# One-hots of the edge targets compared from int32 instead of from bf16 pairs, in a two-layer graph network kernel

## The chip, the cores and the metric

The kernel runs on one core of a Trainium2 chip. The metric is the device time of one execution in microseconds. Three runs of the kernel before gave 11010.66, 11014.35 and 11020.74 us; the median is 11014.35 us. The engines are named as in the profile: PE multiplies matrices, DVE, ACT and POOL work on vectors, SP issues DMAs. POOL also issues the indirect gathers.

## The reference

There are 12,500 nodes with 16 features and 412,500 edges, sorted by target. Two layers follow each other, each closed by a residual sum and a layer norm.

```python
# layer 0: 90 relation types, matrices W_rel from 30 bases
h_src = h[src]
e = concat([h_src @ Ws.T, he @ Ws.T, h[dst] @ Ws.T]) @ Wa.T      # one score for each edge
msg = einsum('ei,eio->eo', h_src, W_rel[rel_type]) * e
x = layernorm(x + segment_sum(msg, dst))
# layer 1: 8 edge types, message by a matrix for each type, then a GRU cell
m = segment_sum(einsum('emh,eh->em', A[edge_type], x[src]), dst)
x = layernorm(x + gru(m, x))
```

## The kernel before

Each of the 128 partitions owns a run of consecutive edges. The edges are worked off in 52 chunks of 62 edges for each partition (CHUNK = 62), two chunks to a pair, with two buffers of everything. First a table is built in HBM that holds, for every node and relation type, the transformed row (`relation_table`). Of the 62 edges of a chunk in layer 0, 44 get their row out of that table: POOL issues one indirect DMA for each of these 44 columns (`gather`, L480), which takes one row for each partition by the int32 offsets in `idx`. The other 18 edges (`Layer.share`) are computed: PE multiplies one-hots with the node features and the relation matrices, ACT makes these one-hots, and DVE picks and sums the products (`make_rows`, L1118 to L1132). They come in a first group of two and four groups of four, the five "quads" of a chunk, counted here 0 to 4.

DVE weighs the rows of a chunk with the edge scores and sums over runs of equal targets with scans (`scan`, L1082). In DVE's program the work of chunk n is woven between the quads of chunk n+1 (`with_quad`). At quad 0 stand `target_parts` and `edge_scores`, at quad 1 `weigh_messages`, whose first instruction (the index for chunk n+2, L1015) stands behind the wait for the landed gathers of chunk n. Scans are spread over quads 1 to 4.

The change touches a side computation: a histogram of the targets, which later gives the last row of each node. `target_parts` takes the low 7 bits of the 62 targets (`dst_lo_i`) and the rest (`dst_hi_i`) as int32, and casts both to bf16 (`dst_lo`, `dst_hi`). `target_hots` then compares them with 0, 1, 2, ... (`iota_bf`), for 16 edges at a time (14 in the last), one instruction for the low part, 128 wide, and one for the high part, 98 wide. I call these two instructions a pair of compares. There are four in a chunk, one at each of the quads 1 to 4 (HOT_WITH), and each stands behind that quad's scans. PE multiplies the two one-hots into `ps_hist` (L610). All operands are stored as pairs: the innermost dimension of `hot_lo`, `hot_hi` and `iota_bf` is 2 and runs over two neighbouring edges, so that every operand has two bf16 values side by side.

POOL runs ahead. While DVE works on chunk n, POOL issues the gathers of chunk n+1, and it goes on to chunk n+2 when the offsets of that chunk are set and the buffer is free. Nothing in POOL's program waits for the compares. In the last chunk the four pairs of compares stand one behind the other, before its wait for the gathers.

The order of each engine's instructions is written out by hand; semaphores connect the engines.

Of the kernel before, what the change touches and what calls it, by code (L numbers as in the profile page):

```python
# [41 lines left out]
def build(nc, x, src, dst, edge_attr, type_8, type_90, Ws, Wa, weight, w_comp,  # L42
# [44 lines left out]
    with ctx:  # L87
        def sb(name, shape, dt=F32):
            return ctx.enter_context(nc.sbuf_tensor(name, shape, dt))
# [36 lines left out]
        run_start = sb("run_start", [P, 1], I32)  # L126
        iota_bf = sb("iota_bf", [P, P, 2], BF16)
        zeros_bf = sb("zeros_bf", [P, P], BF16)
# [50 lines left out]
        dst_hi_i = sb("dst_hi_i", [P, CHUNK], I32)  # L179
        dst_lo = sb("dst_lo", [P, CHUNK], BF16)  # L180
        dst_hi = sb("dst_hi", [P, CHUNK], BF16)
        hot_lo = sb("hot_lo", [P, 2, HOT // 2, P, 2], BF16)
        hot_hi = sb("hot_hi", [P, 2, HOT // 2, TILES, 2], BF16)
        ordered = sb("ordered", [P, 4])
# [371 lines left out]
        def _(pe):  # L556
# [49 lines left out]
            def count_edges(i, q):  # L606

                pe.wait_ge(hot_set[q % 2], i * HOTS + q // 2 + 1)
                for k in range(min(HOT, CHUNK - q % HOTS * HOT)):
                    last = pe.matmul(ps_hist[0:TILES, 0:P], hot_hi[:, q % 2, k // 2, :, k % 2],  # L610
                                     hot_lo[:, q % 2, k // 2, :, k % 2],
                                     start=False, stop=False)
                last.then_inc(hot_used[q % 2], 1)
# [318 lines left out]
        def _(dve):  # L932
# [48 lines left out]
            dve.wait_ge(consts_set, 2)  # L981
            dve.tensor_copy(iota_bf[:, :, :], iota_i[:, :].unsqueeze(2).to_broadcast([P, P, 2]))
            dve.tensor_copy(ident_bf[:, :], ident[:, :])
# [177 lines left out]

            STEPS = 5

# [3 lines left out]
            def target_parts(i, h):  # L1167
# [5 lines left out]
                chunk_done(i, h, 1)  # L1173
                dve.tensor_copy(dst_lo[:, :], dst_lo_i[:, :])
                dve.tensor_copy(dst_hi[:, :], dst_hi_i[:, :]).then_inc(chunk_step, 1)
                chunk_done(i, h, 2)

            def target_hots(i, h, q):

                b = (h * HOTS + q) % 2  # L1180
                wait_past(dve, hot_used[b], i * HOTS + (h * HOTS + q) // 2)
                edges = slice(q * HOT, min((q + 1) * HOT, CHUNK))
                twos = (edges.stop - edges.start) // 2
                for hot, part, width in ((hot_lo, dst_lo, P), (hot_hi, dst_hi, TILES)):
                    all_of = [P, twos, width, 2]
                    last = dve.tensor_tensor(hot[:, b, 0:twos, :, :],  # L1186
                                             part[:, edges].rearrange("p (c e) -> p c e", e=2).unsqueeze(2).to_broadcast(all_of),
                                             iota_bf[:, 0:width, :].unsqueeze(1).to_broadcast(all_of), ALU.is_equal)
                last.then_inc(hot_set[b], 1)

            def edge_scores(i, h):
# [3 lines left out]
                                  he_w[:, :].unsqueeze(1).to_broadcast([P, CHUNK, D]), ALU.mult).then_inc(chunk_step, 1)  # L1195
                chunk_done(i, h, 3)
                dve.tensor_reduce(score[:, :], he_dot[:, :, :], AX, ALU.add).then_inc(he_used[h], 1)

            def weigh_messages(i, h):
# [5 lines left out]
                dve.tensor_tensor(score[:, :], score[:, :], rows0[:, h, :, D], ALU.add).then_inc(chunk_step, 1)  # L1205
                chunk_done(i, h, 4)
                dve.tensor_tensor(weighted[:, :, :], rows0[:, h, :, 0:D],
                                  score[:, :].unsqueeze(2).to_broadcast([P, CHUNK, D]), ALU.mult
                                  ).then_inc(chunk_step, 1)
                wait_past(dve, scan0_out[h], i * 16)  # L1210
                chunk_done(i, h, 5)

# [304 lines left out]
```

## Time and profile before

| | |
|---|---|
| median of three runs | 11014.35 us (11010.66 to 11020.74) |
| span of the profiled execution, first to last instruction | 6658.0 us |
| outside the span (median less span) | 4356.35 us |
| PE, PEld busy | 5232.2, 4919.8 us |
| DVE busy | 4394.2 us (66%) |
| ACT busy | 4410.5 us (66%) |
| POOL busy | 5012.1 us (75%) |
| layer 0, the chunks | about 250 to 3590 us of the span |
| layer 1, the chunks | about 3730 to 6500 us |

The profiled execution has no other time of its own than its span; what lies outside (launch and the like) the trace does not show. Busy shares are averages over stages with different limits, so they are to be read by stage. An indirect gather of POOL is one row in the trace; its duration is the time until POOL is through with it, not until the data have landed.

### The profile page before, as it was taken

How to read it: one execution, taken by the hardware profiler on the slowest of the kernel's cores; microseconds unless marked ns; L12 is line 12 of the kernel's file. 1: busy time of each engine (PE TensorE's matmuls, PEld its weight loads, DVE VectorE, ACT ScalarE, POOL GpSimd, SP SyncE). 2: the span in 40 equal slices, each digit the busy share in tenths (PEclk: the TensorE clock that was granted, in tenths of full speed). 3: DMA queues.
4: the chain of work that ended last, by engine and by line, in shares of the span. 5: the costliest groups of instructions: out<-in, count | busy, mean ns of one | idle time of the engine just before them, and what ended most of it. 6: DMA issues, size and time to landing. Idle time of an engine off the chain costs nothing.

```text
span 6658.0 us, 145553 instructions
## 1 busy us (share of the span) xinstructions
PE 5232.2 (79%) x56854; PEld 4919.8 (74%) x56854; DVE 4394.2 (66%) x9230; ACT 4410.5 (66%) x5373; POOL 5012.1 (75%) x4786
## 2 busy tenths in 40 slices
PE   5687786777777778777784889898888988898884
PEld 1476676776777667677673789888888988888883
DVE  2477676676766767667674566676666666666663
ACT  5775665665666566566562678777777877777763
POOL 5477777777777777777776677777777777777776
PEclk7798898888889888888886799999999999999995
DMA  9511111111111111111112121212122122222221
GB/s 309 209 35 26 35 33 27 35 25 35 32 29 35 26 35 32 28 35 25 35 32 44 36 18 17 17 17 18 17 19 19 17 17 17 17 17 18 20 17 13
DMA packets 647456, 248.56 MB, mean 37 GB/s; under 512 B 531458, under 2 KB 620379, under 8 KB 646360
## 3 DMA queue, kind: packets, MB, share of 16 engines
q0 software_dynamic: 152992, 41.40, 7.9%
q10 hardware_dynamic: 421728, 84.39, 7.3%
q1 hardware_dynamic: 72152, 113.41, 5.1%
q8 instruction: 559, 9.16, 0.6%
q14 instruction: 25, 0.20, 0.0%
HBM read 75.13 MB, written 163.34 MB: 36 GB/s over the span
## 4 chain that ended last, share of the span: by engine, by line
POOL 72%; issue 22%; DMA 3%; ACT 1%; DVE 1%; ACTq 0%; POOLq 0%; PE 0%; SPq 0%; DVEq 0%
POOL rows L480 70%; DMA relation_table<-scanned 2%; POOL sums L480 2%; DMA sums<-scanned,group_row 0%; ACT scanned L817 0%; ACTq L806 0%; DMA relation_table<-t_buf 0%; DMA scanned<-scanned 0%; DVE scanned L1082 0%; DMA scanned<-carry,fix_row 0%; DMA x_sb<-in_x 0%; POOLq L478 0%; ACT t_buf L817 0%; DVE whole L966 0%; PE ps_table L752 0%
## 5 line engine op out<-in xcount | busy, mean ns | idle before, releaser
L647 PE MATMUL ps_table<-node_parts,hot_key 128*128 128x192 bf16 (+1 forms) x44928 | 4173.0, 256 | 756.2 <-DVE by_in L1127 750.9
L647 PEld LDWEIGHTS ps_table<-node_parts,hot_key 128*128 128x128 bf16 x44928 | 3970.7, 101 | 843.2 <-DVE by_in L1127 751.8
L845 ACT ACTIVATE hot_key<-ps_misc,less_key 128x512 bf16<-128x512 f16 x3744 | 2214.0, 702 | 1906.3 <-PE ps_misc L623 1901.7
L480 POOL DMA_INDIRECT rows<-relation_table,idx x2288 | 2626.5, 1148 | 773.4 <-issue 697.0
L480 POOL DMA_INDIRECT rows<-type_table,idx x2184 | 2097.1, 960 | 681.7 <-issue 665.2
L850 ACT ACTIVATE hot_key<-hot_key,ones 128x3072 bf16<-128x3072 bf16 (+1 forms) x468 | 1513.9, 3235 | 15.2
L1123 DVE TENSOR_REDUCE source<-picked 128x32 f32<-128x416 f32 x936 | 805.1, 860 | 32.2
L1132 DVE TENSOR_REDUCE rows<-by_in 128x32 f32<-128x512 f32 (+1 forms) x988 | 694.1, 703 | 33.8
L1118 DVE TENSOR_TENSOR picked<-ps_table,hot_tile 128x416 f32<-128x416 f32 x936 | 543.8, 581 | 250.6 <-PE ps_table L657 250.0
L1127 DVE TENSOR_TENSOR by_in<-ps_table,source 128x512 f32<-128x512 f32 (+1 forms) x936 | 660.9, 706 | 32.3
L1140 DVE TENSOR_SCALAR hot_key<-hot_key 128x1024 bf16<-128x1024 bf16 x260 | 117.5, 452 | 680.3 <-ACT hot_type L846 680.3
L1015 DVE SCALAR_TENSOR_TENSOR idx<-src_sb,t_sb 128x44 int32 (+3 forms) x108 | 21.9, 205 | 787.6 <-DMA rows<-relation_table,idx 598.5
L623 PE MATMUL ps_misc<-ident_f,match_cols 128*128 128x128 f16 x3848 | 325.3, 228 | 201.5 <-issue 150.3
L623 PEld LDWEIGHTS ps_misc<-ident_f,match_cols 128*128 128x128 f16 x3848 | 265.4, 102 | 240.0 <-issue 168.6
L1082 DVE TENSOR_TENSOR_SCAN scanned<-cont,scanned,rows 128x62 f32<-128x62 f32 x1664 | 423.9, 327 | 2.0
L657 PE MATMUL ps_table<-rel_mats,hot_type 90*128 90x272 bf16 x2496 | 358.0, 279 | 0.0
L846 ACT ACTIVATE hot_type<-ps_misc,less_type 96x512 bf16<-96x512 f16 (+1 forms) x468 | 330.7, 707 | 0.0
L610 PE MATMUL ps_hist<-hot_lo,hot_hi 128*98 128x128 bf16 x3224 | 223.9, 221 | 66.2 <-DVE hot_hi L1186 66.1
L610 PEld LDWEIGHTS ps_hist<-hot_lo,hot_hi 128*98 128x98 bf16 x3224 | 209.9, 124 | 77.4 <-DVE hot_hi L1186 74.6
L657 PEld LDWEIGHTS ps_table<-rel_mats,hot_type 90*128 90x128 bf16 x2496 | 236.0, 97 | 32.4
L1186 DVE TENSOR_TENSOR hot_lo<-dst_lo,iota_bf 128x2048 bf16<-128x2048 bf16 x208 | 242.5, 1166 | 0.0
L480 POOL DMA_INDIRECT sums<-scanned,group_row x196 | 185.4, 946 | 68.3 <-issue 58.8
(197 smaller groups left out, 2527.5 us busy)
## 6 DMA issues: line engine op xcount, KB each, us to landing
scanned<-scanned ACTq DMA_DIRECT2D x52, 992.0 KB, 3.9
relation_table<-scanned SPq DMA_DIRECT2D x50, 765.0 KB, 6.4
relation_table<-t_buf SPq DMA_DIRECT2D x48, 765.0 KB, 6.5
rows<-relation_table,idx POOLq DMA_INDIRECT x2288
rows<-type_table,idx POOLq DMA_INDIRECT x2184
scanned<-scanned ACTq DMA_DIRECT2D x52, 496.0 KB, 8.3
he<-in_edge_attr SPq DMA_DIRECT2D x52, 434.0 KB
type_table<-t_buf SPq DMA_DIRECT2D x14, 448.0 KB, 3.0
```

The costliest lines, as they stand in the source:

```text
L480: pool.indirect_dma_start(out=rows[:, k, :], out_offset=None, in_=table, in_offset=bass.IndirectOffsetOnAxis(ap=index[:, k:k + 1], axis=0) ...
L610: last = pe.matmul(ps_hist[0:TILES, 0:P], hot_hi[:, q % 2, k // 2, :, k % 2], hot_lo[:, q % 2, k // 2, :, k % 2], start=False, stop=False)
L623: last = pe.transpose(match_bank[:, k, c * P:(c + 1) * P], match_cols[:, parity, k, at:at + 1].to_broadcast([P, P]), ident_f16[:, :])
L647: pe.matmul(ps_table[duo][:, 0, t * BLOCK_W:t * BLOCK_W + width], hot_key[:, b, g, edges], node_parts[:, part, g:TILES:BLOCKS, :], start=( ...
L657: last = pe.matmul(ps_table[duo][:, 1 + t, 0:lay.outs * D], hot[:, edges], mats_part, start=(k == 0), stop=(k == len(lay.mats) - 1))
L845: act.activation(hot_key[:, b, g, :], match_bank[:, 0, :], ACT.Abs, bias=less_key[:, g:g + 1])
L850: last = act.activation(hot_key[:, b, 0:last_block, :], hot_key[:, b, 0:last_block, :], ACT.Relu, bias=ones[:, 0:1], scale=-1.0)
L1082: return dve.tensor_tensor_scan(scanned[:, h, :, at + f], cont[:, :], messages[:, :, f], scanned[:, 1 - h, CHUNK - 1, at + f:at + f + 1], ...
L1118: dve.tensor_tensor(picked[:, :, :, :], ps_table[duo][:, 0, 0:DUO * BLOCK_W].rearrange("p (t j f) -> p t j f", t=DUO, f=D), hot_tile[:, ha ...
L1123: dve.tensor_reduce(source[:, :, :], picked[:, :, :, :].rearrange("p t j f -> p t f j"), AX, ALU.add).then_inc(match_step[lay.n], 1)
L1127: dve.tensor_tensor(by_in[:, :, 0:lay.outs, :], ps_table[duo][:, 1:1 + DUO, 0:lay.outs * D].rearrange("p t (o i) -> p t o i", i=D), source ...
L1132: dve.tensor_reduce(lay.rows[:, half, lay.own + own:lay.own + own + DUO, 0:lay.outs], by_in[:, :, 0:lay.outs, :], AX, ALU.add).then_inc(ro ...
```

## The change

The casts to bf16 and the bf16 iota go. The compares read the int32 parts and the int32 iota that the kernel has anyway, and their outputs are stored edge by edge, still in bf16. The number of compares, their elements and their places stay. PE reads the one-hots with unit stride. The step count of a chunk falls from 5 to 4.

```diff
@@ -177,10 +176,8 @@
         dst_lo_i = sb("dst_lo_i", [P, CHUNK], I32)
         dst_hi_i = sb("dst_hi_i", [P, CHUNK], I32)
-        dst_lo = sb("dst_lo", [P, CHUNK], BF16)
-        dst_hi = sb("dst_hi", [P, CHUNK], BF16)
-        hot_lo = sb("hot_lo", [P, 2, HOT // 2, P, 2], BF16)
-        hot_hi = sb("hot_hi", [P, 2, HOT // 2, TILES, 2], BF16)
+        hot_lo = sb("hot_lo", [P, 2, HOT, P], BF16)
+        hot_hi = sb("hot_hi", [P, 2, HOT, TILES], BF16)
...
                 for k in range(min(HOT, CHUNK - q % HOTS * HOT)):
-                    last = pe.matmul(ps_hist[0:TILES, 0:P], hot_hi[:, q % 2, k // 2, :, k % 2],
-                                     hot_lo[:, q % 2, k // 2, :, k % 2],
+                    last = pe.matmul(ps_hist[0:TILES, 0:P], hot_hi[:, q % 2, k, :], hot_lo[:, q % 2, k, :],
                                      start=False, stop=False)
...
             dve.wait_ge(consts_set, 2)
-            dve.tensor_copy(iota_bf[:, :, :], iota_i[:, :].unsqueeze(2).to_broadcast([P, P, 2]))
...
                 chunk_done(i, h, 1)
-                dve.tensor_copy(dst_lo[:, :], dst_lo_i[:, :])
-                dve.tensor_copy(dst_hi[:, :], dst_hi_i[:, :]).then_inc(chunk_step, 1)
-                chunk_done(i, h, 2)
...
                 edges = slice(q * HOT, min((q + 1) * HOT, CHUNK))
-                twos = (edges.stop - edges.start) // 2
-                for hot, part, width in ((hot_lo, dst_lo, P), (hot_hi, dst_hi, TILES)):
-                    all_of = [P, twos, width, 2]
-                    last = dve.tensor_tensor(hot[:, b, 0:twos, :, :],
-                                             part[:, edges].rearrange("p (c e) -> p c e", e=2).unsqueeze(2).to_broadcast(all_of),
-                                             iota_bf[:, 0:width, :].unsqueeze(1).to_broadcast(all_of), ALU.is_equal)
+                count = edges.stop - edges.start
+                for hot, part, width in ((hot_lo, dst_lo_i, P), (hot_hi, dst_hi_i, TILES)):
+                    all_of = [P, count, width]
+                    last = dve.tensor_tensor(hot[:, b, 0:count, :], part[:, edges].unsqueeze(2).to_broadcast(all_of),
+                                             iota_i[:, 0:width].unsqueeze(1).to_broadcast(all_of), ALU.is_equal)
```

On DVE, the start of a chunk's side work before the change (quad 0 of the first pair; `dst_lo_i` and `dst_hi_i` are the int32 parts of the targets):

```order
L1170 TENSOR_SCALAR dst_lo_i<-dst_sb 128x62
L1171 TENSOR_SCALAR dst_hi_i<-dst_sb 128x62
L1174 CAST dst_lo<-dst_lo_i 128x62
L1175 CAST dst_hi<-dst_hi_i 128x62
L1076 SCALAR_TENSOR_TENSOR cont<-dst_sb,ordered 128x62
L1194 TENSOR_TENSOR he_dot<-he,he_w 128x992
L1197 TENSOR_REDUCE score<-he_dot 128x62
```

The same place on DVE after the change:

```order
L1165 TENSOR_SCALAR dst_lo_i<-dst_sb 128x62
L1166 TENSOR_SCALAR dst_hi_i<-dst_sb 128x62
L1071 SCALAR_TENSOR_TENSOR cont<-dst_sb,ordered 128x62
L1185 TENSOR_TENSOR he_dot<-he,he_w 128x992
L1188 TENSOR_REDUCE score<-he_dot 128x62
```

Two instructions a chunk are gone, and the lines behind have moved up by five and more. The second place is quad 1 on DVE, with the first pair of compares (`hot_lo`, `hot_hi`) between the scans and the next picked rows, before:

```order
L1207 TENSOR_TENSOR he_dot<-rows,score 128x992
L1082 SCALAR_TENSOR_TENSOR scanned<-cont,scanned,rows 128x62 x4
L1186 TENSOR_TENSOR hot_lo<-dst_lo,iota_bf 128x2048
L1186 TENSOR_TENSOR hot_hi<-dst_hi,iota_bf 128x1568
L1118 TENSOR_TENSOR picked<-ps_table,hot_tile 128x416
L1123 TENSOR_REDUCE source<-picked 128x32
```

The same place on DVE after the change:

```order
L1198 TENSOR_TENSOR he_dot<-rows,score 128x992
L1077 SCALAR_TENSOR_TENSOR scanned<-cont,scanned,rows 128x62 x4
L1178 TENSOR_TENSOR hot_lo<-dst_lo_i,iota_i 128x2048
L1178 TENSOR_TENSOR hot_hi<-dst_hi_i,iota_i 128x1568
L1113 TENSOR_TENSOR picked<-ps_table,hot_tile 128x416
L1118 TENSOR_REDUCE source<-picked 128x32
```

The compares keep their places and sizes and read the int32 tiles; POOL's, ACT's, SP's and PE's instructions stand in the same order as before.

## Rows read from the trace of the kernel before

**Rows 1.** The page: span, and the chain that ended last, by line.
```profile
span 6658.0 us, 145553 instructions
...
POOL rows L480 70%; DMA relation_table<-scanned 2%; POOL sums L480 2%; DMA sums<-scanned,group_row 0%; ACT scanned L817 0%; ACTq L806 0%; DMA relation_table<-t_buf 0%; DMA scanned<-scanned 0%; DVE scanned L1082 0%; DMA scanned<-carry,fix_row 0%; DMA x_sb<-in_x 0%; POOLq L478 0%; ACT t_buf L817 0%; DVE whole L966 0%; PE ps_table L752 0%
```

**Rows 2.** Groups by shape, POOL's gathers: count | busy us, mean ns | idle before
```profile
L480 POOL DMA_INDIRECT rows<-relation_table,idx x2288 | 2626.5, 1148 | 773.4 <-issue 697.0 <-DMA relation_table<-scanned 76.4
L480 POOL DMA_INDIRECT rows<-type_table,idx x2184 | 2097.1, 960 | 681.7 <-issue 665.2 <-DMA type_table<-t_buf 16.4
```

**Rows 3.** Timeline, DVE, first instruction behind the gathers' landing, in consecutive chunks
```profile
2039.69 0.20 DVE L1015 SCALAR_TENSOR_TENSOR idx<-src_sb,t_sb 128x44 int32 x1 [14.68 <-DMA rows<-relation_table,idx]
...
2103.97 0.20 DVE L1015 SCALAR_TENSOR_TENSOR idx<-src_sb,t_sb 128x44 int32 x1 [7.92 <-DMA rows<-relation_table,idx]
```

**Rows 4.** Waits over the span: engine, line <- releaser: us, times, longest
```profile
PE ps_table L647 <- DVE by_in L1127: 750.9, 78, 16.7
...
DVE idx L1015 <- DMA rows<-relation_table,idx: 598.5, 50, 16.0
...
DVE picked L1118 <- PE ps_table L657: 250.0, 164, 13.9
```

**Rows 5.** Groups by shape, DVE's compares of the targets and one cast
```profile
L1186 DVE TENSOR_TENSOR hot_lo<-dst_lo,iota_bf 128x2048 bf16<-128x2048 bf16 x156 | 187.1, 1200 | 0.0
...
L1186 DVE TENSOR_TENSOR hot_hi<-dst_hi,iota_bf 128x1568 bf16<-128x1568 bf16 x156 | 150.9, 967 | 0.0
...
L1186 DVE TENSOR_TENSOR hot_lo<-dst_lo,iota_bf 128x1792 bf16<-128x1792 bf16 x52 | 55.3, 1064 | 0.0
...
L1186 DVE TENSOR_TENSOR hot_hi<-dst_hi,iota_bf 128x1372 bf16<-128x1372 bf16 x52 | 44.9, 864 | 0.0
...
L1174 DVE CAST dst_lo<-dst_lo_i 128x62 bf16<-128x62 int32 x52 | 13.6, 261 | 1.8
```

**Rows 6.** Groups by shape, DVE's other two-tensor instructions, 32-bit operands
```profile
L1194 DVE TENSOR_TENSOR he_dot<-he,he_w 128x992 f32<-128x992 f32 x52 | 61.6, 1184 | 0.0
...
L1098 DVE TENSOR_TENSOR hot_tile<-match_i,iota_i 128x234 f32<-128x234 int32 x52 | 20.6, 396 | 0.0
```

**Rows 7.** Timeline (start, duration), a gather beside one f32 product of DVE
```profile
2019.70 1.18 DVE L1194 TENSOR_TENSOR he_dot<-he,he_w 128x992 f32<-128x992 f32 x1
...
2020.26 1.44 POOL L480 DMA_INDIRECT rows<-relation_table,idx  x1 [0.30 <-issue]
```

**Rows 8.** Timeline, a free gather, then gathers beside the chunk's four compare pairs
```profile
2010.87 0.94 POOL L480 DMA_INDIRECT rows<-relation_table,idx  x1 [0.30 <-issue]
2012.12 2.86 POOL L480 DMA_INDIRECT rows<-relation_table,idx  x1 [0.30 <-issue]
...
2042.31 1.20 DVE L1186 TENSOR_TENSOR hot_lo<-dst_lo,iota_bf 128x2048 bf16<-128x2048 bf16 x1
2042.42 2.80 POOL L480 DMA_INDIRECT rows<-relation_table,idx  x1 [0.30 <-issue]
2043.43 0.97 DVE L1186 TENSOR_TENSOR hot_hi<-dst_hi,iota_bf 128x1568 bf16<-128x1568 bf16 x1
...
2053.15 2.67 POOL L480 DMA_INDIRECT rows<-relation_table,idx  x1 [0.30 <-issue]
...
2060.51 0.59 DVE L1118 TENSOR_TENSOR picked<-ps_table,hot_tile 128x416 f32<-128x416 f32 x1 [2.60 <-PE ps_table L657]
...
2064.88 4.33 POOL L480 DMA_INDIRECT rows<-relation_table,idx  x1 [0.30 <-issue]
```

**Rows 9.** Timeline, a compare of f32 output from int32, and the gather beside it
```profile
2112.06 0.40 DVE L1098 TENSOR_TENSOR hot_tile<-match_i,iota_i 128x234 f32<-128x234 int32 x1
2112.30 0.97 POOL L480 DMA_INDIRECT rows<-relation_table,idx  x1 [0.30 <-issue]
```

**Rows 10.** Timeline of the last chunk: the last of four compare pairs in a row
```profile
3561.82 1.08 DVE L1186 TENSOR_TENSOR hot_lo<-dst_lo,iota_bf 128x1792 bf16<-128x1792 bf16 x1
...
3562.14 1.58 POOL L480 DMA_INDIRECT rows<-relation_table,idx  x1 [0.30 <-issue]
```

More of the change, by code:

```diff
@@ L126, in build @@
         run_start = sb("run_start", [P, 1], I32)
-        iota_bf = sb("iota_bf", [P, P, 2], BF16)
         zeros_bf = sb("zeros_bf", [P, P], BF16)
@@ L1158, in chunk_rows @@
                         between(q)
-            STEPS = 5
+            STEPS = 4
             def chunk_done(i, h, k):
@@ L1195, in edge_scores @@
                                   he_w[:, :].unsqueeze(1).to_broadcast([P, CHUNK, D]), ALU.mult).then_inc(chunk_step, 1)
-                chunk_done(i, h, 3)
+                chunk_done(i, h, 2)
                 dve.tensor_reduce(score[:, :], he_dot[:, :, :], AX, ALU.add).then_inc(he_used[h], 1)
@@ L1205, in weigh_messages @@
                 dve.tensor_tensor(score[:, :], score[:, :], rows0[:, h, :, D], ALU.add).then_inc(chunk_step, 1)
-                chunk_done(i, h, 4)
+                chunk_done(i, h, 3)
                 dve.tensor_tensor(weighted[:, :, :], rows0[:, h, :, 0:D],
@@ L1210, in weigh_messages @@
                 wait_past(dve, scan0_out[h], i * 16)
-                chunk_done(i, h, 5)
+                chunk_done(i, h, 4)
             def scan_some(h, some):
```

## The prediction

> **What bounds the kernel now.** I read the chain that ended last first. POOL's gathers at L480 are 70% of it; the reader is to see that no other line has more than 2% [rows 1]. So layers 0 and 1 go at the pace at which POOL gets through its indirect gathers. Then the groups by shape: a gather of layer 0 takes 1148 ns in the mean and one of layer 1 takes 960, and POOL is idle in front of them for 697.0 us over 2288 gathers, 0.305 us each, which nothing but the issue itself explains [rows 2]. So POOL never waits for DVE once it has begun; a chunk of layer 0 should take 44 times (0.94 + 0.305), about 55 us. The timeline says 64.3 us from one landing to the next (2039.69 to 2103.97) [rows 3]. Where do the missing 9 us go?
>
> The timeline beside single gathers answers that. A free one takes 0.94 us. Those that run into a pair of compares take 2.86, 2.80, 2.67 and 4.33 [rows 8]. Take the second: the gather starts at 42.42 (of 2042.42), `hot_hi` ends at 43.43 + 0.97 = 44.40, and the gather ends at 45.22, 0.82 later. The same arithmetic holds for a plain f32 product: it ends at 2019.70 + 1.18 = 2020.88 and the gather at 2021.70, again 0.82 later [rows 7]. I read this so: about 0.12 us after its start a gather needs something that DVE holds during an instruction with two inputs in SBUF; it gets it when DVE's instruction ends, and then needs its last 0.82 us. Of the four pairs, a pair delays one gather by 1.92, 1.86, 1.73 and 3.39 us in the rows shown, 8.9 us a chunk. From the groups: 2288 x (1148 - 944) ns is 467 us, 9.0 us a chunk, and the f32 product adds 0.5 of it in the chunk of rows 7. So the compares cost POOL, and thereby the kernel, some 8 us a chunk, 415 us in all, though DVE itself has time to spare.
>
> DVE waits 598.5 us for gathers, 11.5 us a chunk, and 250.0 us for PE; PE waits 750.9 us for DVE [rows 4]. Those engines are not the bound: their chain takes 64 - 11.5 = 52.5 us of a chunk's 64.
>
> **The change part by part.** *The compares' own time.* In bf16 pairs, 2048 elements take 1200 ns and 1792 take 1064, so 0.53 ns an element; 1568 and 1372 take 967 and 864 [rows 5]. No row shows these shapes from int32 with a bf16 output. The nearest is `hot_tile`, also an is_equal of an int32 part against the int32 iota with the same kind of broadcast, f32 out: 234 elements in 396 ns; the f32 product takes 1184 ns for 992 [rows 6]. Between the two the slope is 788/758 = 1.04 ns an element with 153 ns fixed. I take this line: 2048 elements 2.28 us, 1568 1.78, 1792 2.02, 1372 1.58. A full pair grows by 1.08 + 0.82 = 1.90 us, the short one by 0.95 + 0.72 = 1.67, a chunk by 3 x 1.90 + 1.67 = 7.37 us. Lower bound: the old time (growth 0, if the 16-bit output let it run at 0.53). [...] All 32-bit rows lie on the line, so I take it.
>
> [...]
>
> *What lies beside other work.* On DVE itself the 7.37 us fall into its wait of 11.5 us for the gathers. Two casts of 0.26 us or less go, about 0.5 us a chunk, into the same wait [rows 5]. DVE and PE would need 52.5 + 7.4 - 0.5 = 59.4 us a chunk, under the present 64. If POOL's cover were gone this would be the period. PE counts the edges behind the fourth pair, so it may wait up to 1.7 us more there once a chunk; it idles for 750.9 us anyway.
>
> *What lies on the path.* A pair outlasts the period of a gather, 1.25 us, both before (2.08 us with the overlap of its two) and after (3.98 us), so one gather is always caught, and is let go at the pair's end. Every us that the pair gets longer is a us that this gather gets longer, and all later ones start later. So POOL's chunk grows by the full 7.37 us, to 71.4, above the 59.4 of DVE and PE. In 51 chunks this is 376 us. In the last chunk the four pairs stand in a row and gathers slip through between them (below): I take 3 us for it. Bounds for this holding: none (0) and whole (379 us).
>
> *Phase.* How long a gather is caught depends also on where it stands when the scans and the pair begin. The third pair holds one for 3.39 us, since it is caught in the scans ahead of it. In front of that pair DVE waits 2.60 us for PE [rows 8]; with two longer pairs, less PE's own delay by the first, some 1.9 us of this wait go, so the meeting point moves. If the third pair then held only as the others do (1.84 before the growth), that is 1.55 x 52 = 81 us less; if the fourth were caught early as well, 1.47 x 52 = 76 us more. Nothing tells which; the third is now near the worst case, so I take a quarter of the loss, -20 us.
>
> *Startup.* The iota cast goes: under 1 us, taken as nothing. PE's reads of the one-hots are now of unit stride, off the path either way. Layer 1 has no compare and stays.
>
> Sum: 376 + 3 - 20 = 359 us. The span goes from 6658 to 7017 us. Laid onto the median, with the 4356 us outside the span unchanged: 11014 + 359 = 11373 us.
>
> [...]
>
> **The rivals.** *A, gathers slip through between `hot_lo` and `hot_hi`.* In the last chunk a gather started at 3562.14 and took 1.58 us, so it was let go at 3562.90, the end of `hot_lo` (61.82 + 1.08), not of `hot_hi` [rows 10]. If the longer compares left that gap each time, the next gather would start inside the pair and only the rest of `hot_hi` would hold it: one period of 1.25 us is saved in each of the 204 other pairs, 255 us, and 359 - 255 = 104 us remain: 11118 us. Against: in all four pairs of rows 8 the gather was held to the end of the second compare.
>
> *B, the time hides.* The compares' growth falls into DVE's 11.5 us and POOL is held no longer than now. For: the chain charges DVE with almost nothing, and the stall does not appear as a wait anywhere. It needs holds of a fixed length; the f32 product's hold followed its own end. 11014 us.
>
> [...]
>
> [...]
>
> **How the numbers follow.** Forecast 77%, A 10%, B 5%, C 5%, D 3%. The forecast's own range is 359 with the phase from -81 to +76 (less the -20 taken): 298 to 455, so 11310 to 11470, and somewhat lower for a mixture with A. With A's 11118 and a margin for its phase the range reaches from 11100 to 11460. B, C and D are left out. A difference within 0.2% (22 us) can't be told from none. Slower: the forecast, A and D, 90%. Same: B, 5%. Faster: C, 5%.
>
> **What would show it.** After the change: (1) `hot_lo` of 2048 in 2.28 us and `hot_hi` of 1568 in 1.78; (2) the mean gather of layer 0 at 1148 + 7.37/44 us = 1.31 us, that of layer 1 at 0.96; (3) 71 us between landings; (4) DVE's wait for gathers still about 11 us a chunk; (5) caught gathers of 4 to 5 us, which end 0.82 us behind a pair. I am wrong if caught gathers end behind `hot_lo` (A), keep their length (B), or are 0.94 beside the compares with POOL waiting for offsets or buffers (C).

## The result and the profile after

Before: 11015.53 us (4 runs, 11010.66 to 11020.74). After: **11211.7 us** (4 runs, 11197.34 to 11216.88). The ratio is 1.018, interval 1.0165 to 1.0194: slower by 196 us, clear of the noise, where 359 us had been forecast.

The first thing to read is the span of the page after, and its chain by engine:

```profile
span 11215.1 us, 145400 instructions
...
PE 26%; another core or an unknown queue 26%; issue 24%; DVE 21%; ACT 2%; DMA 1%; DVEq 0%; ACTq 0%; POOL 0%; SPq 0%; POOLq 0%
```

The span is 11215.1 us, and the timed run it belongs to took 11216.88 us: 1.8 us lie outside the span, not 4356. And POOL, 70% of the chain of before [rows 1], has 0% here. So the trace of before had caught an execution of another kind: 6658 us, where the timed runs took 11014. The unchanged kernel, run again with a profile (the first experiment below), shows the same two things:

```profile
span 11020.7 us, 145553 instructions
...
PE 50%; issue 41%; ACT 4%; another core or an unknown queue 3%; DMA 1%; DVE 1%; SPq 0%; POOL 0%; ACTq 0%; DVEq 0%; POOLq 0%
```

So both kernels have **two levels**. Before took 11026 and 11223 us on two chips and 6657 and 6650 us on two others; on each of them all its executions lie within 0.2% of their median. Each chip was used in one session only, so the record can't tell a property of the chip from one of the session; nor does it name the chip of the trace of [rows 1] or of the first timed runs. Ratios and differences below are between kernels on one chip. Only after's trace of the upper level stands beside traces from a chip that may be another, on which before takes nearly the same (11026 us for 11016).

*What the upper level is.* Both kinds have the same instructions, but in the upper one PE slows down once in nearly every one of the 104 chunks. Timeline of after, PE inside such a stretch (start and duration in us; in brackets the idle time before, which nothing but PE's own issue explains):

```profile
2557.62 0.28 PE L653 MATMUL ps_table<-rel_mats,hot_type 90*128 90x272 bf16 x1 [0.44 <-issue]
2558.34 0.28 PE L653 MATMUL ps_table<-rel_mats,hot_type 90*128 90x272 bf16 x1 [0.44 <-issue]
2559.04 0.28 PE L653 MATMUL ps_table<-rel_mats,hot_type 90*128 90x272 bf16 x1 [0.43 <-issue]
```

Here one matmul starts every 0.70 us. Each lasts 0.28 us, no longer than its kind does in the trace of before (0.28 us in the mean), and PE idles 0.44 us in front of it: the matmuls themselves are not slower, they come later. Further into the stretch the steps are of 0.70 or of 1.4 us. Cut a chunk of layer 0 into three: PE at full pace beside the first gathers, the slow stretch, and the rest. Of after:

```profile
core 0: us, PE busy (x) PEld busy (x) DVE busy (x) ACT busy (x) POOL busy (x), PEclk, DMA share, GB/s
2531.00:2556.00 25.00, 20.53 (x229) 19.17 (x227) 23.80 (x40) 14.75 (x20) 20.51 (x13) 0.93 0.15 46
2556.00:2601.00 45.00, 9.50 (x32) 3.17 (x32) 0.00 (x0) 4.46 (x3) 29.71 (x32) 0.54 0.11 18
2601.00:2631.00 30.00, 26.54 (x276) 25.07 (x276) 29.07 (x53) 19.61 (x24) 0.22 (x1) 0.89 0.01 2
```

Of before at the same level (first experiment), the same three:

```profile
1787.00:1815.00 28.00, 22.36 (x217) 20.28 (x215) 19.92 (x38) 13.68 (x20) 22.51 (x19) 0.82 0.22 60
1815.00:1852.00 37.00, 6.54 (x20) 1.97 (x19) 0.00 (x0) 6.40 (x6) 24.09 (x26) 0.54 0.10 8
1852.00:1880.00 28.00, 27.00 (x301) 25.95 (x301) 25.48 (x53) 19.20 (x23) 0.20 (x1) 0.93 0.00 1
```

In the middle part of after PE has 32 matmuls and 32 weight loads in 45 us, one instruction per 0.70 us in the mean, where it does 229 and 227 in the 25 us ahead. DVE has none. POOL alone goes on, a gather each 1.25 us. In the last third POOL is idle and PE, DVE and ACT catch up. The gathers of the next chunk wait for that, so POOL now has a wait that [rows 2] did not have:

```profile
L477 POOL DMA_INDIRECT rows<-relation_table,idx x2288 | 2598.0, 1135 | 2684.5 <-DVE scanned L1077 1821.1 <-issue 682.0 <-DMA relation_table<-scanned 181.3
```

The granted clock is 0.54 in the middle part and 0.93 and 0.89 beside it; over the span it is 0.720 in after and 0.715 in before at this level, against 0.874 in the execution of [rows 1]. The stretches with gathers are not all of the difference: before's first gather of layer 0 starts at 355.9 us here for 252.8 in [rows 1]'s trace, and between the gathers of the two layers lie 272.4 us for 164.0.

*What of the prediction shows directly.* The compares by shape, answering to [rows 5]:

```profile
L1178 DVE TENSOR_TENSOR hot_lo<-dst_lo_i,iota_i 128x2048 bf16<-128x2048 int32 x156 | 353.6, 2266 | 0.0
L1178 DVE TENSOR_TENSOR hot_hi<-dst_hi_i,iota_i 128x1568 bf16<-128x1568 int32 x156 | 278.3, 1784 | 0.0
L1178 DVE TENSOR_TENSOR hot_lo<-dst_lo_i,iota_i 128x1792 bf16<-128x1792 int32 x52 | 103.9, 1999 | 0.0
L1178 DVE TENSOR_TENSOR hot_hi<-dst_hi_i,iota_i 128x1372 bf16<-128x1372 int32 x52 | 82.1, 1579 | 0.0
```

And the gathers that they catch, answering to [rows 8], in the chunk of the windows above (timeline: start, duration):

```profile
2531.83 5.82 POOL L477 DMA_INDIRECT rows<-relation_table,idx  x1 [35.47 <-DVE scanned L1077]
2532.86 2.27 DVE L1178 TENSOR_TENSOR hot_lo<-dst_lo_i,iota_i 128x2048 bf16<-128x2048 int32 x1
2535.04 1.79 DVE L1178 TENSOR_TENSOR hot_hi<-dst_hi_i,iota_i 128x1568 bf16<-128x1568 int32 x1
...
2544.25 4.55 POOL L477 DMA_INDIRECT rows<-relation_table,idx  x1 [0.30 <-issue]
...
2594.22 0.95 POOL L477 DMA_INDIRECT rows<-relation_table,idx  x1 [0.31 <-issue]
...
2630.78 5.82 POOL L477 DMA_INDIRECT rows<-relation_table,idx  x1 [35.62 <-DVE scanned L1077]
```

The first gather starts while the scans ahead of the pair still run (until 2532.95), and is held through them and through the pair: it ends at 2537.65, 0.82 us behind the end of `hot_hi` at 2536.83. Only two of a chunk's four pairs meet gathers here; the other two start at 2606.73 and 2619.23, while POOL stands idle. Over the whole trace 100 of the 208 pairs meet gathers, and each of these has a gather that ends 0.81 to 0.83 us behind it.

### The profile page after: what moved, and what is told of

It is laid out like the page before. It is cut to its first block, busy times and chain, and to the rows that moved or that the text cites. A ratio compares the mean times of both kernels' runs of the same rounds, so it can differ in the third digit from the quotient of the medians.

```text
span 11215.1 us, 145400 instructions
## 1 busy us (share of the span) xinstructions
PE 6092.2 (54%) x56854; PEld 5053.0 (45%) x56854; DVE 4745.5 (42%) x9125; ACT 4412.5 (39%) x5373; POOL 4952.6 (44%) x4786
## 4 chain that ended last, share of the span: by engine, by line
PE 26%; another core or an unknown queue 26%; issue 24%; DVE 21%; ACT 2%; DMA 1%; DVEq 0%; ACTq 0%; POOL 0%; SPq 0%; POOLq 0%
PE ps_table L643 22%; DVE scanned L1077 3%; DVE hot_lo L1178 3%; DVE hot_hi L1178 3%; DVE source L1118 3%; DVE by_in L1122 3%; DVE picked L1113 2%; PE ps_table L653 2%; PE ps_misc L619 1%; DVE rows L1127 1%; ACT hot_key L841 1%; DMA relation_table<-scanned 1%; DVE he_dot L1198 1%; DVE he_dot L1185 1%
## 5 line engine op out<-in xcount | busy, mean ns | idle before, releaser
L643 PE MATMUL ps_table<-node_parts,hot_key 128*128 128x192 bf16 (+1 forms) x44928 | 4838.0, 262 | 3832.5 <-issue 3660.9
L643 PEld LDWEIGHTS ps_table<-node_parts,hot_key 128*128 128x128 bf16 x44928 | 4048.0, 102 | 4550.6 <-issue 4286.1
L477 POOL DMA_INDIRECT rows<-relation_table,idx x2288 | 2598.0, 1135 | 2684.5 <-DVE scanned L1077 1821.1
L477 POOL DMA_INDIRECT rows<-type_table,idx x2184 | 2065.4, 946 | 3194.5 <-DVE scanned L1077 2513.2
L619 PE MATMUL ps_misc<-ident_f,match_cols 128*128 128x128 f16 x3848 | 367.6, 235 | 343.0 <-issue 292.2
L653 PE MATMUL ps_table<-rel_mats,hot_type 90*128 90x272 bf16 x2496 | 425.4, 296 | 224.2 <-issue 222.9
L1178 DVE TENSOR_TENSOR hot_lo<-dst_lo_i,iota_i 128x2048 bf16<-128x2048 int32 x208 | 457.5, 2200 | 0.0
L1178 DVE TENSOR_TENSOR hot_hi<-dst_hi_i,iota_i 128x1568 bf16<-128x1568 int32 x208 | 360.4, 1733 | 0.0
L607 PE MATMUL ps_hist<-hot_lo,hot_hi 128*98 128x128 bf16 x3224 | 257.8, 232 | 158.0 <-DVE hot_hi L1178 108.6
```

Source lines behind the costliest of these rows:

```text
L477: pool.indirect_dma_start(out=rows[:, k, :], out_offset=None, in_=table, in_offset=bass.IndirectOffsetOnAxis(ap=index[:, k:k + 1], axis=0) ...
L619: last = pe.transpose(match_bank[:, k, c * P:(c + 1) * P], match_cols[:, parity, k, at:at + 1].to_broadcast([P, P]), ident_f16[:, :])
L643: pe.matmul(ps_table[duo][:, 0, t * BLOCK_W:t * BLOCK_W + width], hot_key[:, b, g, edges], node_parts[:, part, g:TILES:BLOCKS, :], start=( ...
L653: last = pe.matmul(ps_table[duo][:, 1 + t, 0:lay.outs * D], hot[:, edges], mats_part, start=(k == 0), stop=(k == len(lay.mats) - 1))
L1178: last = dve.tensor_tensor(hot[:, b, 0:count, :], part[:, edges].unsqueeze(2).to_broadcast(all_of), iota_i[:, 0:width].unsqueeze(1).to_bro ...
```

## The experiments

Times of kernels are medians. "A chunk" is a chunk of layer 0. Its parts are medians over the chunks of one trace unless called means: the gathers' time from the first to the last; in it the *hold*, the sum of what gathers take over 0.945 us; then the time until PE is back at full pace; and the *rest* from there to the next gathers. The recorded expectations speak of the runs by their labels: e1 to e6 are the experiments 1 to 6, e8, e9, e10 and e11 the experiments 7 to 10, e13 and e14 the experiments 11 and 12. "Kernel 9" is the kernel of experiment 9.

**1. Before, unchanged.**

> The kernel before, unchanged. The trace of after has a span of 11215 us and in each of the 104 chunks one stretch of 43 to 53 us in which PE issues one instruction every 0.70 us; the trace of before that I predicted from has a span of 6658 us and no such stretch. Theory S (the stretches belong to every timed execution of both kernels, and the trace of before was of an execution without them): the span is about 11013 us, with some 103 stretches, POOL idles 30 us or more a chunk in front of its gathers for DVE's scans, and a chunk of layer 0 takes about 95 us (98.9 less 196/52 = 3.8). Rival O (the 4356 us lie outside the span, and the change brought the stretches): the span is 6658 us again, without stretches.

11027.49 us against 11026.26, ratio 1.0001 (0.999 to 1.0011), span 11020.7. So the timed level belongs to the program, not to what lies around it, and the trace of [rows 1] shows a different level. A chunk is 94.9 us: gathers 59.2 with 4.6 of hold (both means), the stretch ending 5.9 behind the last gather, rest 29.5. In after it is 98.9: gathers 63.4 with 8.7 of hold, 5.8, rest 29.65. By the means a chunk takes 3.9 us more, which is 195 us in 50 chunks. Summed over layer 0, the gathers take 199 us more than in experiment 1's trace, and POOL's long waits in front of them (over 0.5 us) are the same, 2002.5 us for 2002.9. So the 196 us stand in the gathers, and there they are hold.

**2 and 3. Only the pairs 1 and 2 from int32; only the pairs 3 and 4.** Both are before with

```
+        INTS = (0, 1)        # the third experiment: (2, 3)
...
+                    if q in INTS:
+                        all_of = [P, count, width]
+                        last = dve.tensor_tensor(ones_of(hot, b, width)[:, 0:count, :],
+                                                 part_i[:, edges].unsqueeze(2).to_broadcast(all_of),
+                                                 iota_i[:, 0:width].unsqueeze(1).to_broadcast(all_of), ALU.is_equal)
+                        continue
```

> Only the first and second pair of compares of each chunk (at quads 1 and 2) read int32 in the layout of after; the third and fourth stay bf16 pairs; the casts stay. Theory D (DVE and PE take turns, and only pairs between which PE has nothing left to do are on the path): after is 196 us or 3.8 us a chunk slower, two pairs' growth of 1.9; the first pair stands behind the slow stretch where PE waits 2.6 us for it, so this gets one full growth and perhaps half of the second: +100 to +150 us. Theory P (my prediction: every pair holds a gather and POOL is the bound): half of 196, +98 us, each pair the same.

> The mirror: only the third and fourth pair read int32. Theory D: the rest of the 196 us, +50 to +100 us, with PE's waits for the fourth pair 1.7 us longer. Theory P: +95 us (3.57 of 7.37 parts of 196).

Both expectations missed: they had +98 to +150 us for pairs 1 and 2, and +50 to +100 for pairs 3 and 4. Pairs 1 and 2: 11041.84 us, ratio 1.0013 (1.0004 to 1.0023), +16. Pairs 3 and 4: 10994.51, ratio 0.9967 (0.9955 to 0.998), so 32 us *faster*. Pairs 3 and 4 do what they should to the gathers (63.9 us a chunk, hold 9.25), but the rest falls from 29.5 to 25.6 us and takes the loss back. Together the two parts make -16 us, the whole change +196: at this level costs do not add.

**4. All four pairs from int32, the pair layout and the casts kept.**

```
-                for hot, part, width in ((hot_lo, dst_lo, P), (hot_hi, dst_hi, TILES)):
+                for hot, part, width in ((hot_lo, dst_lo_i, P), (hot_hi, dst_hi_i, TILES)):
...
-                                             iota_bf[:, 0:width, :].unsqueeze(1).to_broadcast(all_of), ALU.is_equal)
+                                             iota_i[:, 0:width].unsqueeze(2).unsqueeze(1).to_broadcast(all_of), ALU.is_equal)
```

> All compares read int32, but write the one-hots in the pair layout of before, so that PE reads them with a stride of two as before; the casts and the bf16 iota stay, unused. Theory L (the layout that PE reads costs or gives nothing): within 0.3% of after, ratio 1.018 against before. Rival (PE's unit stride gives back part of it): slower than after, 1.02 or more. Rival (the scattered 16-bit writes of DVE cost more): hot_lo over 2.3 us, 1.02 or more.

11087.27 us, ratio 1.0047 (1.0029 to 1.0065), +61: under what any of its theories said. `hot_lo` takes 2267 ns in the mean, for 2266 in after, so writing in pairs costs DVE nothing here. Gathers 63.8 us and hold 9.2 (after: 63.4 and 8.7); the rest is near 29.7 us in every second chunk and mostly about 26 in the others.

The four kernels at this level side by side, each trace against that of experiment 1, in us:

| | POOL's time in gathers, layer 0 | POOL's long waits, layer 0 | whole span |
|---|---|---|---|
| pairs 1 and 2 | +58 | -54 | +7 |
| pairs 3 and 4 | +246 | -255 | -10 |
| all, layout and casts kept | +272 | -203 | +75 |
| after | +199 | 0 | +194 |

The first column is the hold, and it is paid in all four. What differs is how much of it the waits give back.

**5. Compares of two elements.** This kernel leaves out all but two elements of each compare, and with them nearly all of the histogram. It and the next three ran on a chip at the lower level (before: 6656.96 us), so what they were expected to say of the upper level stays open.

```
+                    last = dve.tensor_tensor(hot[:, b, 0, 0, :], part[:, q * HOT:q * HOT + 2], iota_bf[:, 0, :],
+                                             ALU.is_equal)
```

> From before: each compare works on 2 elements in place of 1372 to 2048, so the histogram is wrong from here on; all waits, casts and PE's 62 products a chunk stay. It asks what the compares cost in timed executions. Model M, from the traces of the unchanged kernel run again and of after: a chunk of layer 0 = time from the first to the last gather (55.0 us + what DVE's instructions hold, 4.6 in before, 8.7 in after) + 5.8 us until PE's slow stretch ends + the rest until DVE has scanned the rows and the next gathers start (29.2 and 29.7 us). With M and a hold of some 0.8 us the gathers take 56 us; the rest is PE's left-over work of 28 us or more and shrinks little: period 90 to 92.5 us, -110 to -240 us. Rival P (my prediction, POOL always busy): the hold of 8 us a chunk goes, -415 us. Rival Z (the compares cost nothing, 11026 us, and after's 196 us come from the new layout alone).

6340.04 us, ratio 0.9526 (0.951 to 0.9542). The hold falls from 9.2 to 1.8 us a chunk and the period from 64.2 to 56.7. The chunks of layer 0 take 378 us less; the prediction had put the compares' cost before any change at 415. Between the gathers of the two layers 57 us more pass, 221 for 164, which was not looked into, and 317 us remain as the gain of the whole.

**6. The weighing, some scans and the first pair moved to quad 0.**

```
-        HOT_WITH, COUNT_WITH = ((), (0,), (1,), (2,), (3,)), ((), (), (0,), (1,), (2, 3))
+        HOT_WITH, COUNT_WITH = ((0,), (), (1,), (2,), (3,)), ((), (), (0,), (1,), (2, 3))
...
-            SCAN_WITH = (range(0), range(4), range(4, 12), range(12, 24), range(24, 2 * D))
+            SCAN_WITH = (range(4), range(4, 8), range(8, 16), range(16, 24), range(24, 2 * D))
```

> From before, bf16 pairs as they are: the weighing of the landed rows, 4 scans and the first pair of compares move from quad 1 to quad 0 in DVE's program, so in front of DVE's long wait for PE's slow stretch, and the scans of the rows end one quad earlier (at quad 2), which lets the next gathers start earlier. Theory D (DVE's chain sets the rest of the chunk behind the slow stretch): 4.9 us of DVE work hide in the 5.8 us between the gathers' end and the end of the slow stretch, -250 us or more. Rival W (PE's left-over work sets it): the next gathers start earlier but the slow stretch starts earlier too, by the same time, and within 0.5% of before.

6609.6 us, ratio 0.9932 (0.9916 to 0.9949). The hold is 8.2 us in place of 9.2. This order shifts the hold by 1 us a chunk; that the pairs are there at all makes most of it, by experiment 5.

**7. The gathers cut in two bursts,** the second from the 23rd on, behind PE's first products of quad 1.

```
+            CUTS = (((22, 1, 0),), ())
...
+                            pool.wait_ge(products_ps[lay.n],
+                                         i * (2 * lay.duos) + lay.done(h, q, duo))
```

> From before: in layer 0 POOL issues 22 of a chunk's 44 gathers and then waits until PE has finished the first products of quad 1 of that chunk, before it issues the other 22. Layer 1 is unchanged. Theory G (PE's slow stretch is tied to the gathers: it begins 6 to 20 us after they begin and ends 5.8 us behind the last): the stretch of 45 us breaks into two of some 13 us, or ends 6 us behind the 22nd gather, and a chunk gets 10 to 20 us shorter, 10000 to 10500 us in all. Rival I (the stretch belongs to a place in PE's instruction stream or in its loop and only happens to lie beside the gathers): it stays 45 us long while POOL stands still, and the chunk gets longer by the wait, slower than 11100 us.

6658.26 us, ratio 1.0004 (0.9994 to 1.0014). In the trace the 23rd gather waits 3.4 us in the first chunk, and in the other 51 no longer than without the edit, 0.3 us. It was meant to break the slow stretches; the chip had none, so it tells nothing of them. A miss.

**8. After, with the two casts put back.**

```
+                dve.tensor_copy(dst_lo[:, :], dst_lo_i[:, :])
+                dve.tensor_copy(dst_hi[:, :], dst_hi_i[:, :]).then_inc(chunk_step, 1)
```

> From after: the two casts of the target parts to bf16 and their wait stay (0.5 us a chunk), only nobody reads them. With e4 (int32 compares in the pair layout, casts kept, +61 us) this tells what the 150 us between e4 and after are: if the layout that PE reads, this is at after's time, 1.018 of before or 0.5 us a chunk more; if the missing casts, which move DVE's work against the slow stretch, it is near e4, 1.005.

7053.24 us, ratio 1.0599 (1.0581 to 1.0616), **+396 us**.

**9 and 10. After again, and after with its iota in PSUM.** A second chip at the lower level (before: 6649.77 us). The tenth kernel keeps int32 targets and unpacked outputs, but one of the two inputs, the iota, is no longer in SBUF; it lies as f32 in PSUM, the memory that PE writes to. For that the compares have moved behind DVE's wait for the products of the bank in which the iota lies, so their place in DVE's program differs too.

```
+        iota_ps = ps_table[1][:, 1, 512 - P:512]
...
                     dve.wait_ge(products_ps[lay.n], lay.done(m, q, duo))
+                    if duo == 1:
+                        owned(q)
...
-                                             iota_i[:, 0:width].unsqueeze(1).to_broadcast(all_of), ALU.is_equal)
+                                             iota_ps[:, 0:width].unsqueeze(1).to_broadcast(all_of), ALU.is_equal)
```

> The kernel after, unchanged. The kernel before has now been timed at two levels: about 11015 to 11026 us, with PE's slow stretches, and 6657 us, without them. At 11015 us the change cost 196 us. At 6657 us only the variant with the casts kept has run, +396 us. Theory P (without the slow stretches POOL is the bound and each us that a pair of compares grows holds a gather one us longer; the casts lie in DVE's wait): where before takes 6657 us, after takes 7040 to 7055 us, ratio 1.058 to 1.060. Rival (the casts matter there too): more than 10 us off e9's 7053. Where before takes 11020 us: 1.018 again.

> From after: the iota that the compares read lies in a free part of one of PE's product banks in PSUM (as f32), so each compare has only one input in SBUF; for that the pairs of compares move behind DVE's wait for the second products of their quad. Where before takes 6657 us: theory H (what holds a gather is an instruction with two inputs in SBUF, however long it takes) has the hold fall from 16.8 us a chunk to 1 to 2 us though the compares last 2.3 and 1.8 us; POOL would need 56.5 us a chunk and DVE with PE, whose wait gets longer by the pairs, 58 to 62: 6350 to 6600 us. Rival T (it is the length of DVE's instruction that counts, or its writes): the hold stays near 16 us and the time near 7050. Where before takes 11020 us: model M has the gathers' time fall from 63.4 to 57 us and the rest grow by up to 4: 10850 to 11100 us.

After: 7039.75 us, ratio 1.0587 (1.0569 to 1.0604), **+390 us**. With the iota in PSUM: 6287.42, ratio 0.9454 (0.9438 to 0.947), 362 us *under* before and 752 under after. That is faster even than the 6350 to 6600 us that theory H gave. The groups of after and then of the PSUM kernel:

```profile
L477 POOL DMA_INDIRECT rows<-relation_table,idx x2288 | 3006.8, 1314 | 773.1 <-issue 696.9 <-DMA relation_table<-scanned 76.2
```

```profile
L479 POOL DMA_INDIRECT rows<-relation_table,idx x2288 | 2254.6, 985 | 773.7 <-issue 697.0 <-DMA relation_table<-scanned 76.8
...
L1182 DVE TENSOR_TENSOR hot_lo<-dst_lo_i,ps_table 128x2048 bf16<-128x2048 int32 x156 | 353.0, 2263 | 3.2 <-PE ps_table L655 3.2
```

The compare itself is as long as with two SBUF inputs (2263 ns for 2266), only the gathers go free. One pair in the timeline of after:

```profile
2025.96 2.27 DVE L1178 TENSOR_TENSOR hot_lo<-dst_lo_i,iota_i 128x2048 bf16<-128x2048 int32 x1
2026.07 4.68 POOL L477 DMA_INDIRECT rows<-relation_table,idx  x1 [0.30 <-issue]
2028.14 1.79 DVE L1178 TENSOR_TENSOR hot_hi<-dst_hi_i,iota_i 128x1568 bf16<-128x1568 int32 x1
```

And one of the PSUM kernel:

```profile
2018.48 2.26 DVE L1182 TENSOR_TENSOR hot_lo<-dst_lo_i,ps_table 128x2048 bf16<-128x2048 int32 x1
2018.59 0.94 POOL L479 DMA_INDIRECT rows<-relation_table,idx  x1 [0.30 <-issue]
2019.84 0.94 POOL L479 DMA_INDIRECT rows<-relation_table,idx  x1 [0.30 <-issue]
2020.66 1.78 DVE L1182 TENSOR_TENSOR hot_hi<-dst_hi_i,ps_table 128x1568 bf16<-128x1568 int32 x1
2021.09 0.94 POOL L479 DMA_INDIRECT rows<-relation_table,idx  x1 [0.30 <-issue]
```

Both gathers start 0.11 us behind `hot_lo`. The first takes 4.68 us and ends at 2030.75, 0.82 behind the pair's end (2029.93); the second takes 0.94. The same holds over both traces. In kernel 9 all 208 pairs are followed by the end of a gather, 0.81 to 0.83 us behind them. In kernel 10's layer 0 a compare runs 0.11 us behind the start of 572 gathers (119 in kernel 9, half of them of 4.55 us or more), and the longest of the 572 takes 0.96 us. So the moved place of the compares does not explain it: they meet more gathers than in kernel 9 and hold none.

**11 and 12. The second and the tenth kernel on a chip at the upper level** (before: 11222.69 us).

> The kernel of e2 (from before; only the first and second pair of a chunk read int32), which cost 14 us where before takes 11026. Where before takes 6650 us: theory P has each pair's growth on POOL, 2 x 1.90 us x 51 chunks = 194 us, half of after's 390. Rival (after's cost lies in the later pairs or is not additive): under 120 or over 270 us. Where before takes 11020 us: +14 us again, and then this says only that e2 repeats.

> The kernel of e11, run again for its time on another chip if it comes to one. Where before takes 6650 us: 0.945 again. Where before takes 11020 us: model M, 0.985 to 1.007.

Pairs 1 and 2 from int32: 11161.24 us, ratio 0.9942 (0.9925 to 0.9958), so -61 us here and +16 on the first chip. The PSUM kernel: 11714.08, ratio 1.0435 (1.0418 to 1.0453), *slower* by 491 us, where model M gave 0.985 to 1.007, and with the gathers freer than anywhere:

```profile
L479 POOL DMA_INDIRECT rows<-relation_table,idx x2288 | 2220.1, 970 | 3473.7 <-DVE scanned L1079 2610.0 <-issue 681.7 <-DMA relation_table<-scanned 182.0
```

```profile
1731.00:1741.00 10.00, 8.32 (x99) 7.80 (x98) 8.35 (x13) 9.08 (x11) 7.87 (x8) 1.00 0.07 5
1741.00:1794.00 53.00, 9.12 (x34) 3.73 (x34) 4.32 (x12) 0.52 (x1) 34.59 (x37) 0.54 0.14 26
1794.00:1840.00 46.00, 37.77 (x406) 35.15 (x405) 39.24 (x65) 29.69 (x35) 0.03 (x1) 0.86 0.05 13
```

These are the three parts of one of its chunks, under the same headings as above. The same of kernel 11, on the same chip:

```profile
1723.00:1744.00 21.00, 17.58 (x211) 16.23 (x208) 19.72 (x38) 14.72 (x20) 17.34 (x13) 1.00 0.19 55
1744.00:1789.00 45.00, 10.64 (x38) 3.56 (x36) 0.00 (x0) 4.48 (x3) 29.65 (x32) 0.51 0.13 18
1789.00:1819.00 30.00, 26.59 (x296) 25.16 (x297) 29.16 (x53) 20.08 (x24) 0.29 (x1) 0.94 0.01 2
```

The slow stretch begins 10 us behind the first gather of kernel 12 and 21 behind that of kernel 11. So PE has done less by then, 99 matmuls for 211, and has 406 left for the time behind it, for 296. By the medians the gathers are 4.4 us shorter than in kernel 11 (55.8 for 60.2), the stretch ends 6.4 us behind the last gather (for 5.9), the rest is 14.2 us longer (44.0 for 29.8), and the chunk takes 106.2 us for 95.8. These two kernels differ in more than the gathers, though. In kernel 12 the compares stand behind DVE's wait for PE, and three of the four pairs fall into the rest, where kernel 11 has two; all four are int32, the outputs are unpacked and the casts gone. After did not run on this chip, so how much of the loss comes from the free gathers and how much from the place of the compares was not separated.

## Why the prediction was right and wrong

**The mechanism: right.** A compare with both inputs in SBUF holds a gather until it ends, and the gather ends 0.82 us later. The kernels 9 and 10 show it: a compare of the same length (2266 and 2263 ns), one input elsewhere, and the mean gather goes from 1314 to 985 ns. It takes both inputs in SBUF: with the iota in PSUM none of 572 gathers beside a compare took over 0.96 us. Compares of 16-bit parts at 0.53 ns an element [rows 5, rows 8] and of 32-bit parts at 1.1 ns both do it. The 0.12 us of the prediction shows at DVE's f32 products (`he_dot`) in the trace of [rows 1]. The 82 gathers that start inside a product, 0.21 us or more before its end, all end 0.81 to 0.82 us behind that end. The 5 that start 0.11 us before the end take 0.94, as free ones do, and so do 87 in which the product begins 0.18 us or more behind their start (0.96 at most). Between the two, a gather that starts 0.16 us before the end of an int32 compare takes 0.97 us and ends 0.81 behind it [rows 9]. What it is that DVE holds no trace names; that stays the prediction's reading.

**The sizes: right, at the level they were read from.** By the prediction's own points:
1. `hot_lo` 2266 ns (2.28 forecast), `hot_hi` 1784 (1.78), the short ones 1999 and 1579 (2.02 and 1.58).
2. Mean gather of layer 0 1314 ns (1.31), of layer 1 962 (0.96).
3. The two landings here are 71.85 us apart (71):

```profile
2023.35 0.20 DVE L1010 SCALAR_TENSOR_TENSOR idx<-src_sb,t_sb 128x44 int32 x1 [11.75 <-DMA rows<-relation_table,idx]
...
2095.20 0.20 DVE L1010 SCALAR_TENSOR_TENSOR idx<-src_sb,t_sb 128x44 int32 x1 [17.51 <-DMA rows<-relation_table,idx]
```

4. DVE's wait for gathers 737.7 us, 14.2 a chunk and not 11: rather than fill that wait, the change made it longer. POOL's chunk grew by 7.4 us and DVE's work by 6.9 (7.4 less the casts), and DVE waited less for PE, 149.0 us in place of 250.0 [rows 4], 1.9 a chunk; so by this sum 2.4 more were left to wait for gathers, and 2.7 were measured. An error without a price, since DVE stayed off the path.
5. Caught gathers of mostly 4.55 us and up to 5.99 (4 to 5 forecast), ending 0.82 behind a pair.

The hold grew from 9.2 to 16.6 us a chunk, 7.4 for the 7.37 of the sum, and the chunks of layer 0 take 380 us more than in the trace of [rows 1]. On the two chips of this level the change (with the casts kept on one) costs 390 and 396 us against the 359. The -20 for the phase did not come: 376 + 3 = 379 without it is within 11 us of 390.

**The step that failed** is the last sentence of the sum: "Laid onto the median, with the 4356 us outside the span unchanged". The timed executions had no such 4356 us; in every profiled run since, 1.8 us or less lie outside the span. They had a slow stretch in nearly every chunk, and POOL stands idle in front of each chunk's gathers, for 35.5 us in the rows above, so "the gathers are the path" holds for part of the chunk only. The sign of it stood beside the span: 11014 us timed, 6658 traced. The sum should have been laid onto the traced execution alone, or given with a second case for the timed one.

**That 11212 us fell into the stated range was luck.** The forecast's own range, 11310 to 11470 us, begins 98 us above it. The stated range reached down to 11100 only for rival A, and A hardly happened: of the 100 pairs that meet gathers in after's trace, 2 let one go at `hot_lo`'s end. The slow stretches, which did bring the time down, stood in no part of the sum.

**Where 163 of the 359 us went.** At the upper level two of the four pairs fall into the part of the chunk where no gather runs. There the windows show PE as busy as DVE: before 27.00 and 25.48 of 28 us, after 26.54 and 29.07 of 30. The growth of pairs 1 and 2, 3.8 us, fills DVE's slack and moves the rest by 0.2 us. Pairs 3 and 4 still meet gathers; their growth of 1.90 + 1.67 = 3.57 us is nearly all of the measured 3.9 a chunk. This says where the time stands in the trace. It is not what a pair costs alone, as experiments 2 and 3 show. With the change the chain that ended last has also moved in part to DVE: PE 50%, issue 41% and DVE 1% in before at this level, PE 26% and DVE 21% in after.

**What kept that from being a rule.** The parts do not add (experiments 2, 3, 4, 11), and 12 turns the sign. What goes with the gains and losses is how much PE gets done before the slow stretch begins and how much it has left behind it. Of some 534 matmuls a chunk, kernel 3 has 265 left and a rest of 25.6 us, before 309 and 29.5, kernel 11 305 and 29.8, kernel 12 410 and 44.0. After has 292 and 29.65, with DVE busy for nearly all of it. A reading that fits, argued from the traces and not tested: a long-held gather at the burst's start leaves PE time for more work before POOL's undisturbed gathers begin, and what PE has not done by then it does later, with POOL idle. Queue q8, which the profile calls `instruction`, may have to do with the stretch itself. Its packets and share of the 16 DMA engines, in the first 25 us of after's chunk:

```profile
q10 hardware_dynamic: 144, 1.02, 9.8%
q0 software_dynamic: 370, 0.10, 4.9%
q8 instruction: 2, 0.03, 0.5%
```

In the 45 us of the slow stretch it has no row at all:

```profile
q0 software_dynamic: 1038, 0.28, 7.3%
q1 hardware_dynamic: 160, 0.51, 3.8%
```

In the 30 us behind it there are three packets again. The same holds for after's layer 0 throughout: none of 49 stretches has such a packet. But in before at this level 17 of 49 have some, in kernel 12 23 of 49, and in layer 1 of each trace 24 of 49, and the stretch goes on all the same. So this is a correlation and no proof. At the lower level, beside the gathers of a 72 us chunk of kernel 9, q8 has 5 packets and there is no stretch; whether it has a part in the stretches of the upper level was not shown.

**The rivals.** A, slipping between the two compares: rare. In kernel 9 each of the 208 pairs holds a gather to its end; only in the last chunk (all 4) and at 8 of the 204 other pairs was one let go at `hot_lo`'s end before that. B, the time hides: at the upper level it looks so for pairs 1 and 2, but not for the reason given (DVE's wait for gathers). C, faster (10775 us) since only the bf16 pairs hold a gather: no, an int32 pair held one for 4.68 us. D, slower (12160 us) with compares at 2.1 ns an element: no, 1.1.

**Open.** What the slow stretch is, and why two chips have it and two have not; kernel 7 was to tell, and met none. Also why experiment 4 is 2.6 us a chunk cheaper than after. It differs in the output's layout and the two casts; its gathers take even more than after's (272 us over experiment 1 for 199), but POOL waits 203 us less. At the lower level the casts make little: 396 us over before with them and 390 without, on two chips.

## What to carry to other kernels

Compare the traced execution's span with the timed runs before anything else; where they differ by far more than the 1.8 us seen here, the trace shows another regime, and a sum over its rows holds for that regime only. Where DVE works beside indirect gathers and these are the bound, try its long two-input instructions with one input in PSUM. That gave 362 us of 6650 here, but the same kernel lost 491 us on a chip with slow stretches, so time it where it is to run. A cost on the engine that is the bound is paid only while that engine runs (in after the growth of pairs 1 and 2, 3.8 us a chunk, moved the rest by 0.2), so ask of each piece which part of the period it falls into.

## What the runs showed of the hardware

- The same program took 6650 us on one chip and 11223 us on another, all runs of each chip within 0.2% of their median. On the slow ones PE starts about one instruction, matmul or weight load, each 0.70 us for 43 to 54 us of a chunk (medians by kernel and layer); the stretch ends 5.4 to 6.4 us behind the last gather in layer 0 and 6.8 to 7.0 in layer 1.
- A gather of 128 rows takes POOL 0.945 us and 0.305 us until the next. Beside a compare or a product of DVE with both inputs in SBUF it is held to that instruction's end plus 0.82 us, and mostly through a second one that follows at once (at 12 of kernel 9's 208 pairs it was let go at the first one's end, and the next was held by the second); beside compares with one input in PSUM none of 572 took over 0.96 us.
- An is_equal of two int32 inputs with a bf16 output takes 2266 ns for 2048 elements, as long as with an f32 input from PSUM (2263).
- Gathers 4.4 us shorter went with a chunk 10.4 us longer (kernels 11 and 12, one chip), though the two differ in the place of the compares too.
